# Graph attention on one core: gathering rows of x in place of a prepared node table, with the gates found per chunk

## The chip, the cores and the metric

The kernel runs on one core of one Trainium2 chip. The metric is the device time of one execution in microseconds (us). The engines are named as the profile names them: PE is TensorE, DVE is VectorE, ACT is ScalarE, POOL is GpSimd and SP is the engine that issues most plain transfers. Two runs of the kernel before took 2842.83 and 2848.6 us, median 2845.72 us.

## The reference, cut to what matters

There are 12,500 nodes with 128 features each and 212,500 edges, sorted by their target node. Each edge has a node whose features it carries (`col`, from dst) and a node into which it is pooled (`row`, from src).

```python
messages = x[col]                                   # 212500 x 128
gate = messages @ W_gate.T + b_gate                 # one number for an edge
h = messages @ W_lin.T + b_lin
g = gate[:, 0]
e = exp(g - segment_max(g, row)[row])
denom = segment_sum(e, row) + 1e-16
pooled = segment_sum((e / denom[row])[:, None] * h, row)
x = layernorm(x + pooled @ W_out.T + b_out)
```

The gate of an edge depends on its carried node alone: it is the same for all edges that carry that node. The kernel before uses this and finds 12,500 gates once. The changed kernel finds one for every gathered row.

## The kernel before, in words

**Keys and sort (about 0 to 480 us).** SP loads src and dst. DVE packs each edge into one 32-bit key, counts the edges of each block of 128 nodes by one-hot matmuls, adds pad keys so that each block is a whole number of tiles of 128 edges, and sorts 128 x 1792 keys by a bitonic network on DVE (lines 743 to 764 are its exchanges, two instructions each). Between phases the keys are transposed: PE transposes (L542), ACT copies the result back from PSUM (L441), and DVE goes on with the copy. ACT handles these copies in program order, behind whatever it was given earlier.

**The node table (beside the sort).** SP loads x into `nodes_sb` (L278). POOL multiplies ten nodes a partition at a time by the gate vector `wg` (L362, ten instructions), ACT sums each product row with an activation whose accumulator is read out (L430, 100 of them, a drain behind each), and adds the gate bias (L434). SP stores rows of 130 floats (128 features, a one, the gate; 520 bytes) to `node_table` in HBM (L282). In ACT's program all this stands ahead of the first copy L441. POOL then blanks the sums (L367).

**The chunk loop.** 1757 tiles of 128 edges are handled in 44 chunks of T = 40 tiles. For chunk i:
- DVE's `prepare(i + 1)` (L702 to L725) unpacks the next chunk's keys, PE transposes them (L552 to L557), and ACT's `copy_prep` (L444 to L450) puts the gather indices `gather_at` and the places into SBUF.
- POOL issues 40 indirect DMAs (L375), one per tile, each of which gathers 128 rows. It waits for `prep_copied` of that chunk and for `gather_buf_free`, since there are two buffers `gathered_rows`, used in turn.
- PE waits for the chunk's rows, then transposes the 40 columns of gates (L572). DVE runs a segmented max over them and forms the exponents (`softmax`, L890 to L912), with small transposes on PE in between, and ACT takes the exponential (`weigh`, L454).
- `add_tiles` (L941): for each tile DVE spreads the weights into a 128 x 128 matrix (L916), PE multiplies it with the gathered rows and their column of ones (L590), and DVE adds the 129 columns into the sums (L922). Four tiles make a batch, and the adds run two batches behind the spreads.

DVE's program is one row of work: `prepare(i + 1)`, `softmax(i)`, `add_tiles(i)`, `prepare(i + 2)`, and so on. The last chunk is handled in two parts of 16 and 24 tiles (`EARLY` = 16). The number of tiles is a bound: what is left over behind the real edges and their pads is filled with the key `LAST_KEY`, whose carried node is node 0.

**The end.** DVE forms the inverse denominators (L986 to L993). Then, in 14 groups of 7 blocks, POOL scales (L399), PE transposes and multiplies with the folded weights (L634), DVE adds x and takes mean and variance, and ACT normalises (L488). SP loads x and stores the result.

Of the kernel before, what the change touches and what calls it, by code (L numbers as in the profile page):

```python
# [78 lines left out]
def check_shapes():  # L79
    assert P * MAIN_COLS + REST_ROWS * REST_COLS == EDGES and NODE_ROWS * NODE_COLS == NODES  # L80
# [9 lines left out]
def graph_attention(nc, x, src, dst, w_lin, b_lin, w_gate, b_gate, w_out, b_out, out):  # L90
    check_shapes()
    with ExitStack() as ctx:
# [22 lines left out]
        gathered_rows = [arena[:, k * T * ROW:(k + 1) * T * ROW].rearrange("p (t f) -> p t f", f=ROW) for k in range(2)]  # L115
        gate_prod = sb("gate_prod", [P, GATE_COLS, FEAT])
        gate_junk = sb("gate_junk", [P, FEAT])
        gate_sum = sb("gate_sum", [P, NODE_COLS])
# [60 lines left out]
        free_at = 2 * T * ROW  # L179
# [17 lines left out]
        gate_rows = bank[4][0:T, 0:P]  # L197
# [73 lines left out]
        def _(sp):  # L271
# [12 lines left out]
            sp.dma_start(skeys[0:1].rearrange("(a n) -> a n", a=1), zero_key[:, :]).then_inc(keys_stored, 16)  # L284
            sp.dma_start(skeys[1 + KEYS:].rearrange("(p n) -> p n", n=P), iota_i[0:TAIL_ROWS, :]).then_inc(keys_stored, 16)
# [125 lines left out]
        def _(act):  # L411
# [643 lines left out]
```

## Time and profile before

| | us |
|---|---|
| median of the two runs | 2845.72 |
| span of the profiled execution | 2844.9 |
| POOL busy | 1748.5 (61%) |
| DVE busy | 1676.2 (59%) |
| PE busy | 1008.8 (35%) |
| ACT busy | 174.1 (6%) |
| gathers L375, 1757 of them, busy | 1675.1, mean 953 ns |
| spreads L916, 1760 of them, busy | 599.0 |
| adds L922, 1760 of them, busy | 605.6 |

The runs are given as whole times, and the profile gives the profiled execution's span, from its first to its last instruction: 2844.9 us, which is 0.8 us below the median of the runs. Busy shares are averages over three stages that have different limits, so they say little alone: DVE is close to full during the sort and at about half in the loop, where POOL is the engine that never rests for longer than 0.3 us. "Idle before" in a row is the time in which that engine did nothing ahead of the instruction, with what ended it behind the arrow. A name with q (DVEq, ACTq) is an engine's sequencer, here a drain that signals.

### The profile page before, as it was taken

Reading aid. Unit: us, or ns where it says so; the run is one execution under the profiler, and the core shown is the slowest. Engines: PE = TensorE matmul, PEld = TensorE weight load, DVE = VectorE, ACT = ScalarE, POOL = GpSimd, SP = SyncE. Lnnn points to the kernel's source line nnn. Section 1 sums busy time; section 2 is a strip of 40 time slices with the busy share of each in tenths; the row PEclk is TensorE's granted clock in tenths of the full one; section 3 lists DMA queues with packets and bytes.
Section 4 is the critical chain, followed back from the end, with each engine's and each line's share of the span. In section 5 each row is a group of like instructions: output and inputs, shape, how many; then the busy total and the mean of one; then the engine's idle time right before and its main releaser. Section 6 shows DMA issues by size and latency. Waiting matters only on the chain.

```text
span 2844.9 us, 25631 instructions
## 1 busy us (share of the span) xinstructions
PE 1008.8 (35%) x5080; PEld 835.6 (29%) x5080; DVE 1676.2 (59%) x5604; ACT 174.1 (6%) x664; POOL 1748.5 (61%) x1792
## 2 busy tenths in 40 slices
PE   3012112225233342433334243342433424333377
PEld 3011111224232232422323233232333323233255
DVE  9969998346455464645546455464655646455454
ACT  0421110000000000000000000000000000000025
POOL 0411002777777777777777777777777777777621
PEclk9999996565566665566656556565655656566566
DMA  3020001222222222222222222222222222223924
GB/s 115 3 92 0 0 0 29 54 54 54 55 53 55 53 55 54 54 55 53 55 53 54 54 54 54 54 53 55 53 55 54 55 53 54 54 54 67 41 50 122
DMA packets 91745, 148.65 MB, mean 52 GB/s; under 512 B 30393, under 2 KB 61970, under 8 KB 91588
## 3 DMA queue, kind: packets, MB, share of 16 engines
q0 software_dynamic: 56224, 117.06, 20.8%
q1 hardware_dynamic: 34767, 31.04, 3.5%
q10 hardware_dynamic: 722, 0.20, 0.0%
q8 instruction: 12, 0.20, 0.0%
q14 instruction: 20, 0.16, 0.0%
HBM read 134.35 MB, written 13.83 MB: 52 GB/s over the span
## 4 chain that ended last, share of the span: by engine, by line
POOL 43%; issue 23%; DVE 17%; PE 7%; DVEq 2%; another core or an unknown queue 2%; ACT 2%; DMA 2%; ACTq 1%; POOLq 0%
POOL arena L375 42%; DVE spread L916 3%; DVE nodes_sb L922 2%; PE bank L590 2%; PE bank L634 2%; DMA arena<-node_table,gather_at 1%; DVE rows_b L751 1%; DVE rows_a L750 1%; DVE rows_a L751 1%; POOL gate_prod L362 1%; DVE rows_b L750 1%; ACT gate_junk L430 1%; DVEq L952 1%; DVE turn_b L751 1%
## 5 line engine op out<-in xcount | busy, mean ns | idle before, releaser
L375 POOL DMA_INDIRECT arena<-node_table,gather_at x1757 | 1675.1, 953 | 790.6 <-issue 530.3
L590 PE MATMUL bank<-arena,spread 128*128 128x129 f32 x3520 | 736.9, 379 | 334.5 <-DVE nodes_sb L922 220.6
L590 PEld LDWEIGHTS bank<-arena,spread 128*128 128x128 f32 x3520 | 642.8, 276 | 424.5 <-DVE nodes_sb L922 291.4
L916 DVE TENSOR_SCALAR spread<-iota_row,place_t,weights 128x128 f32<-128x128 f32 x1760 | 599.0, 357 | 184.7 <-PE bank L590 83.0
L922 DVE SCALAR_TENSOR_TENSOR nodes_sb<-nodes_sb,weights,bank 128x129 f32 x1760 | 605.6, 344 | 55.2 <-PE bank L590 10.5
L894 DVE TENSOR_TENSOR_SCAN run_max<-pen,bank 40x128 f32<-40x128 f32 (+1 forms) x45 | 18.5, 411 | 756.8 <-PE bank L572 756.8
L572 PE MATMUL bank<-ident,arena 128*40 128x128 f32 (+1 forms) x45 | 17.3, 384 | 703.0 <-DMA arena<-node_table,gather_at 703.0
L572 PEld LDWEIGHTS bank<-ident,arena 128*40 128x40 f32 (+1 forms) x45 | 5.4, 119 | 711.0 <-issue 711.0
L552 PE MATMUL bank<-ident,dst_f 40*128 40x40 f32 x44 | 13.1, 297 | 235.7 <-DVEq L725 234.2
L542 PE MATMUL bank<-ident,rows_a 128*128 128x128 f32 x112 | 28.1, 429 | 180.0 <-DVE rows_a L776 144.7
L446 ACT ACTIVATE gather_at<-bank 128x40 int32<-128x40 f32 x44 | 8.9, 203 | 1258.6 <-PE bank L557 1229.2
L399 POOL TENSOR_TENSOR turn_a<-nodes_sb,arena 128x896 f32 (+1 forms) x14 | 23.7, 1697 | 97.2 <-PE bank L626 51.0
L552 PEld LDWEIGHTS bank<-ident,dst_f 40*128 40x128 f32 x44 | 7.9, 179 | 245.1 <-issue 245.1
L542 PEld LDWEIGHTS bank<-ident,rows_a 128*128 128x128 f32 x112 | 21.7, 223 | 186.3 <-DVE rows_a L776 149.4
L751 DVE TENSOR_TENSOR rows_a<-rows_b 128x384 f32<-128x384 f32 (+1 forms) x108 | 71.8, 665 | 0.0
L750 DVE TENSOR_TENSOR rows_b<-rows_a 128x384 f32<-128x384 f32 (+1 forms) x108 | 67.1, 621 | 5.9 <-ACT rows_a L441 4.6
L750 DVE TENSOR_TENSOR rows_a<-rows_b 128x384 f32<-128x384 f32 (+1 forms) x108 | 69.6, 644 | 1.7
L751 DVE TENSOR_TENSOR rows_b<-rows_a 128x384 f32<-128x384 f32 (+1 forms) x108 | 69.4, 642 | 0.0
L454 ACT ACTIVATE weights<-bank 128x80 f32<-128x80 f32 (+2 forms) x45 | 10.6, 236 | 935.2 <-PE bank L582 935.2
L362 POOL TENSOR_TENSOR gate_prod<-nodes_sb,wg 125x1280 f32<-125x1280 f32 x10 | 37.2, 3721 | 43.5 <-ACTq L433 43.5
L634 PE MATMUL bank<-wc_t,arena 128*128 128x128 f32 x196 | 60.1, 398 | 4.6 <-ACTq L477 4.6
L542 PE MATMUL bank<-ident,turn_b 128*128 128x128 f32 x98 | 24.3, 428 | 97.7 <-DVE turn_b L751 97.7
(161 smaller groups left out, 1066.0 us busy)
## 6 DMA issues: line engine op xcount, KB each, us to landing
arena<-node_table,gather_at POOLq DMA_INDIRECT x1757, 20.6
node_table<-nodes_sb SPq DMA_DIRECT2D x1, 6347.7 KB
nodes_sb<-in_x SPq DMA_DIRECT2D x1, 6250.0 KB
rows_a<-in_x SPq DMA_DIRECT2D x13, 448.0 KB, 4.1
out<-rows_b SPq DMA_DIRECT2D x13, 448.0 KB, 3.3
k<-sorted_keys SPq DMA_DIRECT2D x132, 20.0 KB
turn_a<-in_src SPq DMA_DIRECT2D x1, 828.0 KB
turn_b<-in_dst SPq DMA_DIRECT2D x1, 828.0 KB
```

Of the source, the lines that this page charges most:

```text
L362: pool.tensor_tensor(gate_prod[0:NODE_ROWS], node_rows[:, c * GATE_COLS:(c + 1) * GATE_COLS, 0:FEAT], wg[0:NODE_ROWS].unsqueeze(1).to_broa ...
L375: pool.indirect_dma_start(out=gathered_rows[par][:, t, :], out_offset=None, in_=table[:, :], in_offset=bass.IndirectOffsetOnAxis(ap=gather ...
L399: pool.tensor_tensor(pooled[par][:, :, :], here[:, :, 0:FEAT], inv_den[:, bass.ds(g * GB, GB)].unsqueeze(2).to_broadcast([P, GB, FEAT]), A ...
L430: last = act.activation(gate_junk[0:NODE_ROWS], gate_prod[0:NODE_ROWS, n, :], ACT.Copy, accum_out=gate_sum[0:NODE_ROWS, at:at + 1])
L542: last = pe.transpose(ps[:, q:q + P], from_[:, at + q:at + q + P], ident[:, :])
L590: last = pe.matmul(tile_ps(slot), lhsT=spread[:, slot, :], rhs=gathered_rows[par][:, b * BATCH + u, 0:WIDTH], start=True, stop=True)
L634: pe.matmul(to, lhsT=pooled_t[par][:, c, :], rhs=wc_t[:, :], start=True, stop=False)
L750: dve.tensor_tensor(vb[:, :, 0, :], va[:, :, 0, :], va[:, :, 1, :], ALU.min)
L751: step_ends(g, dve.tensor_tensor(vb[:, :, 1, :], va[:, :, 0, :], va[:, :, 1, :], ALU.max))
L916: return dve.tensor_scalar(spread[:, slot, :], iota_row[:, :], place_t[par][:, t:t + 1], weights[par][:, 0, t:t + 1], ALU.is_equal, ALU.mult)
L922: dve.scalar_tensor_tensor(here, here, weights[par][:, 1, t:t + 1], tile_ps(slot), ALU.mult, ALU.add).then_inc(sums_added, 1)
L952: got = nc.values_load_multi_w_load_instructions(offs[par][0:1, b * BATCH:b * BATCH + n], engines=[mybir.EngineType.DVE], min_val=0, max_v ...
```

## The change

The node table is gone: its load, products, sums, bias, store and the waits on them. The gathers read rows of x itself, 512 bytes each. Since these rows have no gate and no one in them, the buffers' column of ones is written once (L349 of the changed kernel), and the gates of a chunk are found when its rows have landed. DVE multiplies all 40 x 128 elements a partition by the gate vector, which it has copied to PSUM, in one instruction (`find_gates`). ACT sums each tile's 129 elements (the 129th is the gate bias, written once) by an activation with an accumulator, with a drain behind each, 40 a chunk (`sum_gates`). PE then transposes the sums where it transposed the gathered column before. The wait for the rows moves from PE to DVE.

```diff
-        table = nc.dram_tensor("node_table", (NODES, ROW), F32).ap()
...
+        gate_terms = arena[:, 14000:14000 + T * WIDTH].rearrange("p (t f) -> p t f", f=WIDTH)
+        gates = sb("gates", [P, T])
...
-            sp.dma_start(node_rows[:, :, 0:FEAT], x.rearrange("(p n) f -> p n f", n=NODE_COLS)).then_inc(x_loaded, 16)
-
-            sp.wait_ge(gates_ready, 1)
-            sp.wait_ge(ones_ready, 1)
-            sp.dma_start(table.rearrange("(p n) f -> p n f", n=NODE_COLS), node_rows).then_inc(table_stored, 16)
...
-            for c in range(NODE_COLS // GATE_COLS):
-                if c > 0:
-                    pool.wait_ge(prod_used, c)
-                pool.tensor_tensor(gate_prod[0:NODE_ROWS], node_rows[:, c * GATE_COLS:(c + 1) * GATE_COLS, 0:FEAT],
-                                   wg[0:NODE_ROWS].unsqueeze(1).to_broadcast([NODE_ROWS, GATE_COLS, FEAT]),
-                                   ALU.mult).then_inc(prod_ready, 1)
-
-            pool.wait_ge(table_stored, 16)
             pool.memset(sums, 0.0).then_inc(sums_blank, 1)
 
             pool.wait_ge(hist_ready, 1)
+            for par in range(2):
+                pool.memset(gathered_rows[par][:, :, FEAT:WIDTH], 1.0)
+            pool.drain().then_inc(ones_ready, 1)
...
-                    pool.indirect_dma_start(out=gathered_rows[par][:, t, :], out_offset=None, in_=table[:, :],
+                    pool.indirect_dma_start(out=gathered_rows[par][:, t, 0:FEAT], out_offset=None, in_=x[:, :],
...
-            for c in range(NODE_COLS // GATE_COLS):
-                act.wait_ge(prod_ready, c + 1)
-                for n in range(GATE_COLS):
-                    at = c * GATE_COLS + n
-                    last = act.activation(gate_junk[0:NODE_ROWS], gate_prod[0:NODE_ROWS, n, :], ACT.Copy,
-                                          accum_out=gate_sum[0:NODE_ROWS, at:at + 1])
-                    act.drain()
-                act.drain().then_inc(prod_used, 1)
-            act.activation(node_rows[:, :, FEAT + 1], gate_sum[0:NODE_ROWS, :], ACT.Identity,
-                           bias=bg[0:NODE_ROWS, 0:1]).then_inc(gates_ready, 1)
+            act.wait_ge(hist_ready, 1)
+            act.activation(gate_terms[:, :, FEAT], bg[:, 0:1].to_broadcast([P, T]), ACT.Copy).then_inc(bias_placed, 1)
...
+            def sum_gates(i, at, n):
+                act.wait_ge(terms_ready, i + 1)
+                for t in range(at, at + n):
+                    act.activation(gate_junk[:, :], gate_terms[:, t, :], ACT.Copy, accum_out=gates[:, t:t + 1])
+                    act.drain()
+                act.drain().then_inc(gates_found, 1)
...
                     copy_prep(2 * j + (par + 1), 1 - par)
+                    sum_gates(2 * j + par, 0, T)
                     weigh(2 * j + par, par)
...
+                pe.wait_ge(gates_found, i + 1)
                 pe.nop(nofuse=True)
-                pe.transpose(gate_rows[0:n], gathered_rows[par][:, 0:n, FEAT + 1], ident[:, :]).then_inc(gates_turned, 1)
+                pe.transpose(gate_rows[0:n], gates[:, 0:n], ident[:, :]).then_inc(gates_turned, 1)
...
-                    pe.wait_ge(rows_gathered[par], 16 * T * j + 16 * T)
...
+            dve.tensor_copy(wg_ps, wg[:, :])
...
+            def find_gates(par, at, n):
+                dve.tensor_tensor(gate_terms[:, at:at + n, 0:FEAT], gathered_rows[par][:, at:at + n, 0:FEAT],
+                                  wg_ps.unsqueeze(1).to_broadcast([P, n, FEAT]), ALU.mult)
+                dve.drain().then_inc(terms_ready, 1)
...
                     prepare(i + 1, j + par, 1 - par)
+                    dve.wait_ge(rows_gathered[par], 16 * T * j + 16 * T)
+                    find_gates(par, 0, T)
                     softmax(i, par)
                     add_tiles(i, i + 1, par, range(NB))
```

Two places show how the engines' instructions stand. The first is DVE at the seam between `prepare(i + 1)` and `softmax(i)` in the loop, before:

```order
L723 TENSOR_SCALAR pen<-differs 40x256
L724 TENSOR_SCALAR goes_on<-pen_tile 40x1
L894 SCALAR_TENSOR_TENSOR run_max<-pen,bank 40x128
L897 SCALAR_TENSOR_TENSOR carry<-tile_pen,carry,bank 1x40
L900 COPY carry_col<-bank 40x1
```

and the same place now:

```order
L706 TENSOR_SCALAR pen<-differs 40x256
L707 TENSOR_SCALAR goes_on<-pen_tile 40x1
L963 ISA
L877 TENSOR_TENSOR arena<-arena,bank 128x40x128
L885 SCALAR_TENSOR_TENSOR run_max<-pen,bank 40x128
L888 SCALAR_TENSOR_TENSOR carry<-tile_pen,carry,bank 1x40
L891 COPY carry_col<-bank 40x1
```

The product over a whole chunk stands between the two, ahead of the scan, and behind it the scan waits for ACT and PE. The second place is ACT in the loop, half an iteration, before:

```order
L446 ACTIVATE gather_at<-bank 128x40
L447 ACTIVATE place_t<-bank 128x40
L448 ACTIVATE offs<-bank 1x40
L449 ACTIVATE tile_pen<-bank 1x40
L453 REGISTER_ALU
L454 ACTIVATE weights<-bank 128x80
```

and now:

```order
L419 ACTIVATE gather_at<-bank 128x40
L420 ACTIVATE place_t<-bank 128x40
L421 ACTIVATE offs<-bank 1x40
L422 ACTIVATE tile_pen<-bank 1x40
L426 REGISTER_ALU
L428 ACTIVATE gate_junk,gates<-arena 128x129 x40
L434 ACTIVATE weights<-bank 128x80
```

Forty summing activations stand between the copies of the next chunk's indices, which they do not delay, and the exponential of this chunk.

## Rows read from the trace of the kernel before

**Rows 1.** The page, part 4: the chain that ended last, by engine
```profile
POOL 43%; issue 23%; DVE 17%; PE 7%; DVEq 2%; another core or an unknown queue 2%; ACT 2%; DMA 2%; ACTq 1%; POOLq 0%
```
**Rows 2.** Timeline of a chunk (start, length, engine, line, idle before and its releaser)
```profile
1234.58 0.39 PE L572 MATMUL bank<-ident,arena 128*40 128x128 f32 x1 [15.50 <-DMA arena<-node_table,gather_at]
1235.00 0.41 DVE L894 TENSOR_TENSOR_SCAN run_max<-pen,bank 40x128 f32<-40x128 f32 x1 [16.73 <-PE bank L572]
...
1265.59 0.35 DVE L706 TENSOR_SCALAR node_i<-k 40x384 int32<-40x384 int32 x1
...
1268.31 0.14 DVE L724 TENSOR_SCALAR goes_on<-pen_tile 40x1 f32<-40x1 f32 x1
...
1269.46 0.18 ACT L449 ACTIVATE tile_pen<-bank 1x40 f32<-1x40 f32 x1
...
1282.06 0.94 POOL L375 DMA_INDIRECT arena<-node_table,gather_at  x1 [0.30 <-issue]
1283.31 0.94 POOL L375 DMA_INDIRECT arena<-node_table,gather_at  x1 [0.30 <-issue]
...
1284.71 0.38 PE L572 MATMUL bank<-ident,arena 128*40 128x128 f32 x1 [15.55 <-DMA arena<-node_table,gather_at]
1285.13 0.41 DVE L894 TENSOR_TENSOR_SCAN run_max<-pen,bank 40x128 f32<-40x128 f32 x1 [16.69 <-PE bank L572]
```
**Rows 3.** Timeline of the table's first products: ACT's sums, and POOL behind ten of them
```profile
77.90 0.31 ACT L430 ACTIVATE gate_junk<-gate_prod 125x128 f32<-125x128 f32 x1 [61.48 <-POOL gate_prod L362]
78.12 0.19 ACT L430 ACTIVATION_READ_ACCUMULATOR gate_junk<-gate_prod 125x1 f32 x1
78.38 0.31 ACT L430 ACTIVATE gate_junk<-gate_prod 125x128 f32<-125x128 f32 x1
...
82.67 2.91 POOL L362 TENSOR_TENSOR gate_prod<-nodes_sb,wg 125x1280 f32<-125x1280 f32 x1 [4.87 <-ACTq L433]
```
**Rows 4.** Timeline of DVE in the sort: first, second and last stretched instruction, and a wait
```profile
74.72 0.56 DVE L750 TENSOR_TENSOR rows_a<-rows_b 128x384 f32<-128x384 f32 x1
75.19 3.03 DVE L751 TENSOR_TENSOR rows_a<-rows_b 128x384 f32<-128x384 f32 x1
...
82.98 3.02 DVE L744 TENSOR_TENSOR rows_b<-rows_a 128x384 f32<-128x384 f32 x1
...
130.46 3.16 DVE L776 TENSOR_SCALAR rows_a<-rows_a,flips 128x1024 f32<-128x1024 f32 x1
...
161.98 0.69 DVE L750 TENSOR_TENSOR turn_b<-turn_a 128x512 f32<-128x512 f32 x1 [25.71 <-ACT turn_a L441]
```
**Rows 5.** Waits of DVE between 200 and 480 us (total, times, longest)
```profile
DVE turn_b L750 <- ACT turn_a L441: 1.3, 3, 0.8
```
**Rows 6.** Timeline of DVE late in the sort: a product-like instruction on 512 elements
```profile
456.91 0.69 DVE L750 TENSOR_TENSOR rows_a<-rows_b 128x512 f32<-128x512 f32 x1
```
**Rows 7.** The page, part 5: instructions with an operand in PSUM (busy, mean ns)
```profile
L922 DVE SCALAR_TENSOR_TENSOR nodes_sb<-nodes_sb,weights,bank 128x129 f32 x1760 | 605.6, 344 | 55.2 <-PE bank L590 10.5
```
**Rows 8.** Timeline: the gates' transpose of chunks 0, 41 and 42
```profile
530.69 0.38 PE L572 MATMUL bank<-ident,arena 128*40 128x128 f32 x1 [32.48 <-DMA arena<-node_table,gather_at]
...
2593.63 0.38 PE L572 MATMUL bank<-ident,arena 128*40 128x128 f32 x1 [16.43 <-DMA arena<-node_table,gather_at]
...
2650.14 0.38 PE L572 MATMUL bank<-ident,arena 128*40 128x128 f32 x1 [22.16 <-DMA arena<-node_table,gather_at]
```
**Rows 9.** Windows near the end (busy of each engine, clock, DMA share, GB/s)
```profile
2600.00:2620.00 20.00, 13.89 (x71) 12.38 (x72) 17.70 (x69) 0.00 (x0) 15.12 (x17) 0.76 0.24 53
...
2640.00:2650.00 10.00, 0.00 (x0) 0.00 (x0) 0.00 (x0) 0.00 (x0) 7.56 (x9) 0.50 0.97 40
```
**Rows 10.** Timeline from chunk 42 to the denominators
```profile
2670.45 2.74 PE L590 MATMUL bank<-arena,spread 128*128 128x129 f32 x12 [10.62 <-issue]
...
2711.76 0.41 DVE L894 TENSOR_TENSOR_SCAN run_max<-pen,bank 40x128 f32<-40x128 f32 x1 [3.88 <-PE bank L572]
...
2733.45 0.25 DVE L986 TENSOR_SCALAR arena<-nodes_sb 128x98 f32<-128x98 f32 x1
```

More of the change, by code:

```diff
@@ L68 @@
 WIDTH = FEAT + 1
-ROW = FEAT + 2
-NODE_ROWS, NODE_COLS = 125, 100
-GATE_COLS = 10
 NEG = -1.0e30
@@ L79, in check_shapes @@
 def check_shapes():
-    assert P * MAIN_COLS + REST_ROWS * REST_COLS == EDGES and NODE_ROWS * NODE_COLS == NODES
+    assert P * MAIN_COLS + REST_ROWS * REST_COLS == EDGES
     assert EARLY % BATCH == 0 and CHUNKS % 4 == 0 and (CHUNKS - 1) * T + EARLY < TILES <= CHUNKS * T and (CHUNKS + 1) * T * P < KEYS + TAIL_ROWS * P
@@ L108, in graph_attention @@
         lohi_b = turn_b.ap().bitcast(BF16)
-        nodes_sb = sb("nodes_sb", [P, 13000])
-        node_rows = nodes_sb[0:NODE_ROWS, 0:NODE_COLS * ROW].rearrange("p (n f) -> p n f", f=ROW)
-        sums = nodes_sb[:, 0:BLOCKS * WIDTH]
+        sums = sb("sums", [P, BLOCKS * WIDTH]).ap()
         arena = sb("arena", [P, 23 * EDGE_COLS // 2 + EDGE_COLS])
@@ L114, in graph_attention @@
         part2_i = arena[:, 23 * EDGE_COLS // 2:23 * EDGE_COLS // 2 + EDGE_COLS].bitcast(I32)
[L115 to L118, printed above, removed]
+        gathered_rows = [arena[:, k * T * WIDTH:(k + 1) * T * WIDTH].rearrange("p (t f) -> p t f", f=WIDTH) for k in range(2)]
+        gate_terms = arena[:, 14000:14000 + T * WIDTH].rearrange("p (t f) -> p t f", f=WIDTH)
+        gates = sb("gates", [P, T])
+        gate_junk = sb("gate_junk", [P, WIDTH])
         wg = sb("wg", [P, FEAT])
@@ L177, in graph_attention @@
         pooled_t = [arena[:, k * HALF:k * HALF + GB * P].rearrange("p (c f) -> p c f", f=P) for k in range(2)]
-        free_at = 2 * T * ROW
+        free_at = 2 * T * WIDTH
         inv_den = arena[:, free_at:free_at + BLOCKS]
@@ L196, in graph_attention @@
         count_ps = bank[6][:, 0:HI * LO]
-        gate_rows = bank[4][0:T, 0:P]
+        gate_rows, wg_ps = bank[4][0:T, 0:P], bank[4][:, 256:256 + FEAT]
         tile_block_ps, tile_pen_ps, tile_max_ps = bank[6][0:1, 256:256 + T], bank[6][0:1, 384:384 + T], bank[5][0:1, 128:128 + T]
@@ L204, in tile_ps @@
             return bank[slot // 2][:, (slot % 2) * 256:(slot % 2) * 256 + WIDTH]
-        src_loaded, dst_loaded, x_loaded, weights_loaded = sem("src_loaded"), sem("dst_loaded"), sem("x_loaded"), sem("weights_loaded")
+        src_loaded, dst_loaded, weights_loaded = sem("src_loaded"), sem("dst_loaded"), sem("weights_loaded")
         iotas_ready, consts_ready = sem("iotas_ready"), sem("consts_ready")
-        prod_ready, prod_used, gates_ready, ones_ready = sem("prod_ready"), sem("prod_used"), sem("gates_ready"), sem("ones_ready")
-        table_stored, keys_stored, zero_ready = sem("table_stored"), sem("keys_stored"), sem("zero_ready")
+        terms_ready, gates_found, ones_ready, bias_placed = sem("terms_ready"), sem("gates_found"), sem("ones_ready"), sem("bias_placed")
+        keys_stored, zero_ready = sem("keys_stored"), sem("zero_ready")
         onehots_ready, hist_ready, spread_ready, counts_ready = sem("onehots_ready"), sem("hist_ready"), sem("spread_ready"), sem("counts_ready")
@@ L344, in _ @@
             sp.wait_ge(stored[1], 16 * (GROUPS // 2 + 1))
-            sp.wait_ge(table_stored, 16)
         @block.gpsimd
@@ L464, in _ @@
                     copy_prep(2 * j + (par + 1), 1 - par)
+                    sum_gates(2 * j + par, 0, T)
                     weigh(2 * j + par, par)
             copy_prep(CHUNKS - 1, 1)
+            sum_gates(CHUNKS - 2, 0, T)
             weigh(CHUNKS - 2, 0)
+            sum_gates(CHUNKS - 1, 0, EARLY)
             weigh(CHUNKS - 1, 1, slice(0, EARLY))
+            sum_gates(CHUNKS, EARLY, T - EARLY)
             weigh(CHUNKS, 1, slice(EARLY, T))
@@ L886, in _ @@
             dve.wait_ge(sums_blank, 1)
+            dve.wait_ge(bias_placed, 1)
+            dve.wait_ge(weights_loaded, 16 * 6)
+            dve.tensor_copy(wg_ps, wg[:, :])
             dve.drain().then_inc(sums_added, 2 * BATCH)
+            def find_gates(par, at, n):
+                dve.tensor_tensor(gate_terms[:, at:at + n, 0:FEAT], gathered_rows[par][:, at:at + n, 0:FEAT],
+                                  wg_ps.unsqueeze(1).to_broadcast([P, n, FEAT]), ALU.mult)
+                dve.drain().then_inc(terms_ready, 1)
             def softmax(i, par, n=T):
@@ L974, in _ @@
             prepare(CHUNKS - 1, CHUNKS // 2 - 1, 1)
+            dve.wait_ge(rows_gathered[0], 16 * T * (CHUNKS // 2))
+            find_gates(0, 0, T)
             softmax(CHUNKS - 2, 0)
             add_tiles(CHUNKS - 2, CHUNKS - 1, 0, range(NB))
+            dve.wait_ge(rows_gathered[1], 16 * T * (CHUNKS // 2 - 1) + 16 * EARLY)
+            find_gates(1, 0, EARLY)
             softmax(CHUNKS - 1, 1, EARLY)
             add_tiles(CHUNKS - 1, CHUNKS, 1, range(EARLY // BATCH))
+            dve.wait_ge(late_gathered, 16 * (TILES - (CHUNKS - 1) * T - EARLY))
+            find_gates(1, EARLY, T - EARLY)
             softmax(CHUNKS, 1)
```

8 lines of the change are left out of this document (2 added, 6 removed).

## The prediction

> **What bounds the kernel now.** I read the chain of waits first. It lies on POOL for 43% and on "issue" for 23% [rows 1]; issue is mostly POOL's 0.30 us between two gathers. So in the loop the pace is POOL's: one gather every 1.25 us, 40 in a chunk, and the reader is to see in [rows 2] that nothing holds it up at a chunk's boundary. Chunk 0's gates are transposed at 530.69 and chunk 41's at 2593.63 [rows 8], which is 50.32 us a chunk.
>
> Then the timeline of one chunk, for what the other engines have to spare. From L894 at 1235.00 to L894 at 1285.13 DVE takes 50.13 us, of which it waits 16.69 for rows; the other 33.44 are its own path (softmax, spreads and adds with their short waits, then `prepare`). More telling is what POOL needs from that path: the indices of chunk i+2 are copied at 1269.46 + 0.18 = 1269.64, and the next chunk's first gather is at 1283.31. The loop has a slack of 13.7 us a chunk. Anything added between landing and `add_tiles` is free up to there, and not beyond.
>
> Third, the sort, where DVE is the pace: it waits 25.71 us once for ACT's first copy, since ACT is busy with the table's sums until then, and some instructions take 3.03 in place of 0.56 us [rows 4].
>
> **What the change removes.** The wait of 25.71 goes, since ACT has only one small instruction ahead of its first copy. Late in the sort such waits are 1.3 us in three [rows 5], so 0.4 stays: 25.3 gained. The stretched instructions number seven, 75.19 the first and 130.46 the last; each begins within half a microsecond of one of POOL's products or runs up to its end, as the one at 82.98 beside the product at 82.67 [rows 3, 4]. Five of 384 elements lose 3.03 - 0.56 = 2.47 us, and I take this for all seven: 17.3 gained. POOL's other work moves early and blocks nobody that waits: the sums are not needed before the loop. Together the loop starts 42.6 us earlier, less about 0.2 for copying the gate vector to PSUM: **42.4**. The bound below is 25 (if the stretching had another cause), above 45. The load of x and the store of the table are hidden by the sort, and cost nothing either way. So chunk 0's rows are there at 530.69 - 42.4 = 488.3.
>
> **What it adds in each chunk**, all in a row between landing and the gates' transpose:
> - The product: 512 elements take 0.69 [rows 6], 384 take 0.56 [rows 4], so 1.02 ns an element and 0.17 fixed; 5120 elements take **5.4**. One operand lies in PSUM. The nearest rows with one are the adds, 344 ns for 129 elements [rows 7], which fit 0.17 + 0.13 plus 0.04; nothing there is slower by the element, but they are too short to exclude it. Bounds 5.3 and, at half the pace, 10.7.
> - The sums: ACT starts one at 77.90 and the next at 78.38; ten with their handover back to POOL take 82.67 - 77.90 = 4.77 [rows 3]. These are the same instruction, accumulator read and drain, on 128 elements instead of 129. Forty take **18.9**. Bounds: if read and drain went on beside the next activation, 0.22 each (78.12 - 77.90), 8.8; if each met a hiccup of 0.1, 23.
> - Handovers DVE to ACT and ACT to PE: about **0.3** over the DMA to PE of before; the transpose's 0.42 (1234.58 to 1235.00) stood inside DVE's wait, and now counts.
>
> DVE's path becomes 33.44 + 0.42 + 5.4 + 18.9 + 0.3 = **58.5 us** a chunk. All but 13.7 of the added 24.6 would be past the slack; but once DVE is late the loop has another law. Gathers of chunk i+2 start when its indices are copied, 1.2 us behind the path's end, and 40 gathers later, 39 x 1.25 + (1284.71 - 1282.06) = 51.4, the rows are there. That ring spans two chunks, so it allows (58.5 + 1.2 + 51.4) / 2 = 55.6 us a chunk. DVE's own path, 58.5, is longer, so it decides: the rows of the next chunk lie there when DVE comes, POOL waits some 8 us a chunk, and the kernel changes from bound by POOL to bound by the chain DVE, ACT, PE, DVE. That gathers might get cheaper with 512 bytes instead of 520 is then worth nothing, and that they might be slowed by up to 5 us a chunk by the product costs nothing.
>
> The Trainium skill, page "ScalarE: Activation LUTs", section "What ACT_TABLE_LOAD costs", puts an activation with immediate scale and bias at 186 ns + 0.833 ns an element, with 93 ns of overlap back to back. By that, 129 elements are an estimated 200 ns and forty 8.0 us, the path would be 47.6, and the loop would keep POOL's pace. The rows above have 0.48 us from start to start, because the accumulator's read and the drain stand between; the page prices neither.
>
> **The loop.** Chunk 42's product starts at 488.3 + 42 x 58.5 = 2945.3.
>
> **The end of the loop.** Before, from chunk 42's transpose to L986 it took 2733.45 - 2650.14 = 83.3 [rows 8, 10]. In it were 3.9 of waiting for the last rows, which go, and 10.6 in which PE stood at "issue" in the middle of chunk 42 [rows 10]. Both go with DMA queues that are full from about 2630: share 0.97 at only 40 GB/s where it was 0.24 at 53 [rows 9]. These are the filler tiles, where all 128 rows of a gather are node 0. Their gathers still come, 37 of them in chunk 43, when DVE begins chunk 42, so I let the 10.6 stand. 128 x 520 bytes at 40 GB/s are 1.7 us a gather, 63 us for them: landed at 2945.3 + 1.2 + 66 = 3013, ahead of their use near 3037. The gates add 24.6 for chunk 42; for 16 tiles 2.3 + 7.6 + 0.3 = 10.2; for 24 tiles 3.3 + 11.4 + 0.3 = 15.0. So 83.3 - 3.9 + 49.8 = 129.2, and L986 is at 3074.5. Behind it nothing changes: 2844.9 - 2733.45 = 111.4.
>
> **Sum:** 3074.5 + 111.4 = 3185.9, against 2844.9 of the same execution: +341. The median of the runs is 0.8 above that span, so 3187 us, 12% slower.
>
> **Rivals.**
> *The sums overlap, and POOL stays the pace* (the other side). If read and drain were hidden, forty sums would be 8.8 and DVE's path 48.4; the ring gives (48.4 + 52.6) / 2 = 50.5 a chunk, 0.2 over today's. It decides at a path of 48.0, which is an added 14. The 42.4 of the sort are gained, 42 x 0.2 = 8 lost, and the end of the loop, where rows of node 0 gate the last part, loses some 29 (the added parts of 24.6, 10.2 and 15.0, less 10.1, 4.0 and 6.1 of hidden reads). About 2841 us, no change. For it: the rule above. Against: the ten sums in 4.77 us, the same instructions. 5%; another 2% that the gain shows, and it is over 2% faster.
> *The product is slow in PSUM, or ACT's sums are slower in the loop than in the prologue.* At half pace the product adds 5.3 a chunk, and hiccups of 0.1 add 4: 44 x 5 = 220, about 3400 us. For it: the price with a long PSUM operand is not in the trace. Against: the adds, and that ACT's sums ran beside DVE and POOL in the table too. 9%.
> *The gathers from x don't bring the rows at the pace of the table's,* so that the ring decides at 58.5 or more: they would have to take 5.8 us a chunk longer. Nothing speaks for it; rows of 512 bytes are less data. 2%.
> *The forecast,* 82%: its own terms give 3155 (no stall of PE, 0.5 us a chunk less) to 3260 (the gain of the sort only 25, 1.3 us a chunk more in handovers and small waits).
>
> The range 3150 to 3265 leaves out 2 in 10. A difference of 2% is 57 us and about what counts as a change here. Slower: 82 + 9 + 2 = 93%; within 2%: 5%; faster: 2%.
>
> **What would show it.** In the profile after: L877 about 5.4 us; L428 at 0.47 us a tile and 18.9 a chunk, ACT busy near 1000 us; DVE waiting for the scan some 20 us a chunk, now for ACT's sums and not for rows; POOL idle about 8 us a chunk behind the index copy; the first gather near 436 in place of 478; no stretched DVE instructions before 135. A chunk pace of 50.5 would make the first rival right, and one of 62 or more the second. What would make me wrong is above all a term of the 58.5, since each tenth of a microsecond in it is worth 4.

## The result

| | kernel before | changed kernel |
|---|---|---|
| median of the runs, us | 2845.72 (2 runs) | 3204.02 (2 runs) |
| ratio, with its 95% interval | 1 | 1.1257 (1.1233 to 1.1281) |
| span of the profiled execution, us | 2844.9 | 3203.2 |
| first gather, us from the start | 478 | 442.2 |
| pace of the loop, us a chunk | 50.32 | 58.60 |
| POOL busy | 61% | 53% |
| ACT busy | 6% | 26% |

The changed kernel is 12.6% slower. The forecast was 3187 us with a range of 3150 to 3265, so it was 17 us too low.

### The profile page after: what moved, and what is told of

Read it like the earlier page. It is cut to its first block, busy times and chain, and to the rows that moved or that the text cites. A ratio compares the mean times of both kernels' runs of the same rounds, so it can differ in the third digit from the quotient of the medians.

```text
span 3203.2 us, 30726 instructions
## 1 busy us (share of the span) xinstructions
PE 997.6 (31%) x5080; PEld 827.3 (26%) x5080; DVE 1908.9 (60%) x5650; ACT 843.4 (26%) x3984; POOL 1707.3 (53%) x1783
## 4 chain that ended last, share of the span: by engine, by line
DVE 37%; issue 23%; ACT 17%; PE 9%; DVEq 6%; ACTq 5%; POOL 2%; DMA 0%; POOLq 0%
ACT gate_junk L428 16%; DVE spread L907 7%; DVE arena L877 7%; DVE sums L913 5%; PE bank L577 5%; ACTq L429 5%; DVEq L943 3%; POOL arena L356 2%; DVE rows_a L733 2%; DVE rows_b L734 2%; DVE rows_a L734 2%; DVE rows_b L733 2%; PE bank L617 1%; DVE turn_b L734 1%; DVE turn_b L733 1%
## 5 line engine op out<-in xcount | busy, mean ns | idle before, releaser
L356 POOL DMA_INDIRECT arena<-in_x,gather_at x1757 | 1670.9, 951 | 1275.1 <-ACTq L423 751.4
L428 ACT ACTIVATE gate_junk<-arena 128x129 f32<-128x129 f32 x1760 | 549.4, 312 | 407.9 <-DVEq L879 278.2
L913 DVE SCALAR_TENSOR_TENSOR sums<-sums,weights,bank 128x129 f32 x1760 | 605.6, 344 | 54.4 <-PE bank L577 10.3
L885 DVE TENSOR_TENSOR_SCAN run_max<-pen,bank 40x128 f32<-40x128 f32 (+1 forms) x45 | 18.5, 412 | 869.6 <-PE bank L559 869.6
L559 PE MATMUL bank<-ident,gates 128*40 128x128 f32 (+1 forms) x45 | 16.9, 375 | 1102.9 <-ACTq L430 1102.9
L428 ACT ACTIVATION_READ_ACCUMULATOR gate_junk<-arena 128x1 f32 x1760 | 327.8, 186 | 0.0
L877 DVE TENSOR_TENSOR arena<-arena,bank 128x5120 f32<-128x5120 f32 (+2 forms) x45 | 241.6, 5370 | 43.8 <-DMA arena<-in_x,gather_at 37.2
L380 POOL TENSOR_TENSOR turn_a<-sums,arena 128x896 f32 (+1 forms) x14 | 23.7, 1699 | 142.1 <-DVEq L988 90.8
L536 PE MATMUL bank<-ident,dst_f 40*128 40x40 f32 x44 | 13.1, 297 | 233.0 <-DVEq L708 231.4
L414 ACT ACTIVATE turn_a<-bank 128x512 f32<-128x512 f32 (+1 forms) x40 | 20.7, 543 | 232.8 <-PE bank L526 232.8
L733 DVE TENSOR_TENSOR rows_a<-rows_b 128x384 f32<-128x384 f32 (+1 forms) x108 | 67.1, 621 | 1.7
L434 ACT ACTIVATE weights<-bank 128x80 f32<-128x80 f32 (+2 forms) x45 | 10.6, 236 | 216.1 <-PE bank L569 216.1
L734 DVE TENSOR_TENSOR rows_a<-rows_b 128x384 f32<-128x384 f32 (+1 forms) x108 | 66.6, 617 | 0.0
```

The costliest lines, as they stand in the source:

```text
L356: pool.indirect_dma_start(out=gathered_rows[par][:, t, 0:FEAT], out_offset=None, in_=x[:, :], in_offset=bass.IndirectOffsetOnAxis(ap=gathe ...
L428: act.activation(gate_junk[:, :], gate_terms[:, t, :], ACT.Copy, accum_out=gates[:, t:t + 1])
L733: dve.tensor_tensor(vb[:, :, 0, :], va[:, :, 0, :], va[:, :, 1, :], ALU.min)
L734: step_ends(g, dve.tensor_tensor(vb[:, :, 1, :], va[:, :, 0, :], va[:, :, 1, :], ALU.max))
L877: dve.tensor_tensor(gate_terms[:, at:at + n, 0:FEAT], gathered_rows[par][:, at:at + n, 0:FEAT], wg_ps.unsqueeze(1).to_broadcast([P, n, FEA ...
L913: dve.scalar_tensor_tensor(here, here, weights[par][:, 1, t:t + 1], tile_ps(slot), ALU.mult, ALU.add).then_inc(sums_added, 1)
```

## The profile after

The page's line of busy times, its chain of waits (part 4) and five of its groups (part 5: busy, mean ns of one, idle before and its releaser):

```profile
PE 997.6 (31%) x5080; PEld 827.3 (26%) x5080; DVE 1908.9 (60%) x5650; ACT 843.4 (26%) x3984; POOL 1707.3 (53%) x1783
...
DVE 37%; issue 23%; ACT 17%; PE 9%; DVEq 6%; ACTq 5%; POOL 2%; DMA 0%; POOLq 0%
...
L356 POOL DMA_INDIRECT arena<-in_x,gather_at x1757 | 1670.9, 951 | 1275.1 <-ACTq L423 751.4
...
L428 ACT ACTIVATE gate_junk<-arena 128x129 f32<-128x129 f32 x1760 | 549.4, 312 | 407.9 <-DVEq L879 278.2
...
L913 DVE SCALAR_TENSOR_TENSOR sums<-sums,weights,bank 128x129 f32 x1760 | 605.6, 344 | 54.4 <-PE bank L577 10.3
L885 DVE TENSOR_TENSOR_SCAN run_max<-pen,bank 40x128 f32<-40x128 f32 (+1 forms) x45 | 18.5, 412 | 869.6 <-PE bank L559 869.6
...
L877 DVE TENSOR_TENSOR arena<-arena,bank 128x5120 f32<-128x5120 f32 (+2 forms) x45 | 241.6, 5370 | 43.8 <-DMA arena<-in_x,gather_at 37.2
```

Read the chain first, against [rows 1]: POOL held 43% of it and now holds 2%. DVE has 37% and ACT, which took no part in the loop's pace, 17%. POOL's gathers cost what they did (951 ns, 953 before). What is new is the idle time ahead of them, 751.4 us released by ACT's index copy. DVE no longer waits for rows: of the 43.8 us ahead of the product, 37.2 are chunk 0's. It waits 869.6 us at the scan L885 instead, and the releaser PE leads on to ACT. The adds L913 have their old 344 ns: DVE's other work did not get slower.

The waits from 700 to 2900 us (in total, times, longest) show the same by the chunk:

```profile
DVE run_max L885 <- PE bank L559: 723.2, 37, 19.5
POOL arena L356 <- ACTq L423: 327.9, 38, 9.2
```

That is 19.5 us of DVE a chunk, and 8.6 us of POOL. The timeline of one chunk, to be laid beside [rows 2]:

```profile
1490.81 5.49 DVE L877 TENSOR_TENSOR arena<-arena,bank 128x5120 f32<-128x5120 f32 x1
1491.44 0.20 ACT L419 ACTIVATE gather_at<-bank 128x40 int32<-128x40 f32 x1 [29.39 <-PE bank L541]
1492.70 0.95 POOL L356 DMA_INDIRECT arena<-in_x,gather_at  x1 [8.01 <-ACTq L423]
...
1500.13 0.31 ACT L428 ACTIVATE gate_junk<-arena 128x129 f32<-128x129 f32 x1
1500.35 0.19 ACT L428 ACTIVATION_READ_ACCUMULATOR gate_junk<-arena 128x1 f32 x1
1500.61 0.31 ACT L428 ACTIVATE gate_junk<-arena 128x129 f32<-128x129 f32 x1
...
1515.43 0.37 PE L559 MATMUL bank<-ident,gates 128*40 128x128 f32 x1 [24.02 <-ACTq L430]
1515.84 0.41 DVE L885 TENSOR_TENSOR_SCAN run_max<-pen,bank 40x128 f32<-40x128 f32 x1 [19.54 <-PE bank L559]
...
1549.53 5.49 DVE L877 TENSOR_TENSOR arena<-arena,bank 128x5120 f32<-128x5120 f32 x1 [0.20 <-issue]
```

The product starts as soon as `prepare` is done: its rows lie there. Then all 40 sums run, 0.47 us each, while DVE and PE stand still, and 24.6 us after the product's start (1490.81 to 1515.43) the gates are transposed. The next product starts after 58.72 us. POOL gets its indices 0.6 us into the product and waits 8.01 for them.

## The experiments

Ratios are against the kernel before, run again beside each group of experiments on the same chip. Its medians there were 2841.07 (the first four experiments), 2842.34 (the next four) and 2844.33 us (the last two); whole times of different groups are compared only roughly. Two theories were to be told apart first: mine, that the path DVE, ACT, PE, DVE sets 58.5 us a chunk and each part of the gates' 24.6 us counts, against a rival in which gathers from x, not the gates, had made the loop slow.

**e1, no gates.** Product, sums and the wait for them are left out. The gates stay zero, so the weights of a target's edges are all equal.

```diff
-                    sum_gates(2 * j + par, 0, T)
...
-                pe.wait_ge(gates_found, i + 1)
...
+                    pe.wait_ge(rows_gathered[par], 16 * T * j + 16 * T)
...
-                    dve.wait_ge(rows_gathered[par], 16 * T * j + 16 * T)
-                    find_gates(par, 0, T)
```

> The changed kernel without its product and its sums: the gates stay zero, so the attention weights are all equal; the table is gone and 512-byte rows of x are gathered as in the change. Theory (the loss is the serial work between landing and the gates' transpose, and nothing else in the change costs): the loop is POOL's again at 50.3 us a chunk, the first gather stays at 442, which is 36 us ahead of the kernel before, and the end of the loop is as before: 2846 - 36 = 2810 us. Rival (gathers from x are slower than from the table, or the moved waits cost): a pace above 50.6 us a chunk and over 2825 us.

Measured: 2805.17 us (2 runs), ratio 0.9871 (0.9852 to 0.9891), 50.36 us a chunk. The page, part 5:

```profile
L356 POOL DMA_INDIRECT arena<-in_x,gather_at x1757 | 1677.0, 954 | 916.9 <-issue 527.2
```

From its first gather on POOL is back to waiting for nothing but its own issue. The gathers from x keep the table's pace, and that rival falls. The run also prices the two halves of the change. Up to the denominators (2733.45 us before, 2699.07 here, 3096.06 in the changed kernel) leaving out the table gains 34.4 us, and the gates lose 397.0. The whole spans differ by 42.5 and 400.8, but 8.1 of the 42.5 lie behind the denominators, where the code is the same (see "Behind it nothing changes" in the account of the prediction). The medians of the runs side by side give 35.9.

**e2, every second sum.** ACT sums 20 of the 40 tiles, which leaves half the gates at zero (the code blanks them once).

```diff
-                for t in range(at, at + n):
+                for t in range(at, at + n, 2):
```

> ACT sums every second tile only; the other gates stay zero. Theory (two limits: DVE's serial path, and a ring over two chunks of path + 52.6): the path falls from 58.7 to 58.7 - 20 x 0.47 = 49.3, and the ring gives (49.3 + 52.6) / 2 = 51.0 us a chunk; in the end of the loop 19 us less than in the changed kernel, some 7 more for landing behind slow filler gathers: about 2866 us. Rival (only the larger of DVE's path and POOL's own 50.3 counts, no ring): a pace of 50.3, and 2838 us. Rival (the sums are not what the loop waits for): 3204 us stays.

Measured: 2885.77 us (2 runs), ratio 1.0155 (1.0135 to 1.0175), 51.49 us a chunk. The timeline, three transposes in a row, and between them two products with the first and the fortieth gather of a chunk:

```profile
1535.85 0.38 PE L559 MATMUL bank<-ident,gates 128*40 128x128 f32 x1 [15.45 <-ACTq L430]
...
1588.32 0.37 PE L559 MATMUL bank<-ident,gates 128*40 128x128 f32 x1 [17.73 <-ACTq L430]
...
1623.55 5.49 DVE L878 TENSOR_TENSOR arena<-arena,bank 128x5120 f32<-128x5120 f32 x1 [1.37 <-DMA arena<-in_x,gather_at]
1624.28 0.94 POOL L356 DMA_INDIRECT arena<-in_x,gather_at  x1 [2.27 <-ACTq L423]
...
1638.66 0.37 PE L559 MATMUL bank<-ident,gates 128*40 128x128 f32 x1 [15.68 <-ACTq L430]
...
1673.26 0.94 POOL L356 DMA_INDIRECT arena<-in_x,gather_at  x1 [0.30 <-issue]
1675.75 5.49 DVE L878 TENSOR_TENSOR arena<-arena,bank 128x5120 f32<-128x5120 f32 x1 [3.35 <-DMA arena<-in_x,gather_at]
```

The path is 58.6 - 20 x 0.47 = 49.2 here, shorter than POOL's 50.3, and still the loop takes 51.5. That is the ring over two chunks: it alternates between 52.5 and 50.3 us, and POOL waits 2.27 once in two chunks. The law is right and its constant was too small. 2 x 51.49 - 49.2 = 53.8, where I had 1.2 + 51.4 = 52.6. These rows show most of the missing 1.2. DVE's path ended at 1623.55 - 1.37 = 1622.18, and the first gather starts 2.10 later, where I had 1.2. The fortieth gather starts 48.98 behind it, where I had 48.75, and the next product 2.49 behind that, where I had 2.65. Together that is 53.6. The run took 20 us more than expected, which is about the 0.49 a chunk over 42 chunks.

**e3, no drain between the sums.** The activation writes its output over its own input instead of `gate_junk`, so nothing has to be waited for between two of them.

```diff
-                    act.activation(gate_junk[:, :], gate_terms[:, t, :], ACT.Copy, accum_out=gates[:, t:t + 1])
-                    act.drain()
+                    act.activation(gate_terms[:, t, :], gate_terms[:, t, :], ACT.Copy, accum_out=gates[:, t:t + 1])
```

> All 40 sums, but without the drain behind each; each activation writes back over its own input in place of a shared scratch row. Theory (the drain and the accumulator's read stand between two activations, 0.47 us from start to start): without the drain 0.40 at best if the read still stands between (0.31 + 0.19 less overlap), a path of 55.9 and 3080 us; if the drain alone held it up, 0.22 each, a path of 48.7, a pace of 50.6 and about 2850 us. Rival (it is the read, not the drain): 0.47 stays and so does 3204 us.

Measured: 2932.26 us (2 runs), ratio 1.0319 (1.0298 to 1.0339), 52.73 us a chunk. The timeline of ACT:

```profile
1500.50 0.29 ACT L428 ACTIVATE arena<-arena 128x129 f32<-128x129 f32 x1
1500.70 0.19 ACT L428 ACTIVATION_READ_ACCUMULATOR arena<-arena 128x1 f32 x1
1500.79 0.29 ACT L428 ACTIVATE arena<-arena 128x129 f32<-128x129 f32 x1
```

From start to start it is 0.29 us, against 0.47 above, which is between the two values that I expected (0.40 and 0.22). So the drain was 0.18 of each sum. The read starts 0.20 behind its activation and takes 0.19, and the next activation starts 0.10 before the read's end. Forty sums are 7.1 shorter, and the ring with the constant measured in e2 gives ((58.6 - 7.1) + 53.8) / 2 = 52.7, as measured. The first rival of the prediction needed 0.22 a sum, and even without drains it is not reached.

**e4, POOL's blanking late.** The prediction let POOL's moved work block nobody. The trace after shows POOL and DVE in the first microseconds otherwise:

```profile
1.65 10.63 POOL L345 MEMSET sums<- 128x12642 f32 x1 [0.16 <-issue]
...
3.20 9.17 DVE L641 CAST iota_row<-iota_i 128x128 f32<-128x128 int32 x1
3.29 9.07 DVE L642 CAST part_idx<-part_idx_i 128x1 f32<-128x1 int32 x1
3.36 9.04 DVE L643 TENSOR_SCALAR diag_eq<-diag_i 64x64 f32<-64x64 int32 x1
...
14.05 1.03 DVE L662 TENSOR_SCALAR rows_b<-turn_a 128x1696 int32<-128x1696 int32 x1
```

Two conversions and a comparison take 9 us, and all end with POOL's memset, at 12.3. They stand one behind the other on DVE, so the rows show that the first was held; the other two may only have stood behind it. In the kernel before the memset stood behind the table, at 211 us. The experiment moves it behind POOL's wait for the histogram:

```diff
-            pool.memset(sums, 0.0).then_inc(sums_blank, 1)
             pool.wait_ge(hist_ready, 1)
+            pool.memset(sums, 0.0).then_inc(sums_blank, 1)
```

> The changed kernel, but POOL blanks the sums behind its wait for the histogram, during the sort's exchanges with two inputs. Theory (the 10.6 us blanking at 1.65 blocked three small DVE instructions until 12.3, and the key packing began at 14.05 instead of 7.16; the same blanking did not stretch the exchanges at 211 us in the kernel before): the first gather at 435.3 instead of 442.2, 6.9 us less, 3197 us. Rival (blanking blocks DVE wherever it stands): no gain, or up to 10 us more.

Measured: first gather at 435.4 instead of 442.2. The median is 3198.75 us (4 runs), ratio 1.1259 (1.124 to 1.1278), which does not tell it from the changed kernel's 1.1257. The gain is shown by the trace alone: chunk 0's product starts at 487.34 instead of 494.27. At the denominators 4.7 us of it are left, since PE's stall in chunk 42 is 13.1 here and 9.85 there. The timeline:

```profile
3.20 0.18 DVE L640 CAST iota_row<-iota_i 128x128 f32<-128x128 int32 x1
...
7.11 1.04 DVE L661 TENSOR_SCALAR rows_b<-turn_a 128x1696 int32<-128x1696 int32 x1 [1.83 <-DMA turn_a<-in_src]
...
52.15 10.63 POOL L346 MEMSET sums<- 128x12642 f32 x1 [50.66 <-PE bank L509]
53.25 0.69 DVE L732 TENSOR_TENSOR rows_b<-rows_a 128x512 f32<-128x512 f32 x1
```

DVE's key packing starts 6.9 us earlier. The same memset beside two-input exchanges of the sort stretches none of them: 0.69 us, as in [rows 6]. The rival, that blanking blocks DVE wherever it stands, falls. The Trainium skill, page "SBUF — State Buffer", section "Who interferes with whom", says that a DVE instruction with two SBUF inputs contends with a GpSimd instruction that reads SBUF, and not with one that only writes it, and that casts and tensor-scalar operations can enter modes that contend. These rows agree with both: the table's products, which read, stretched exchanges to 3.03 us [rows 4], and the memset, which only writes, stretches none.

**e5, the sums on DVE.** One reduction over 40 x 129 elements behind the product, nothing on ACT.

```diff
-                    sum_gates(2 * j + par, 0, T)
...
-                dve.drain().then_inc(terms_ready, 1)
+                dve.drain()
+                dve.tensor_reduce(gates[:, at:at + n], gate_terms[:, at:at + n, :], AX.X, ALU.add)
+                dve.drain().then_inc(gates_found, 1)
```

> The changed kernel, but DVE sums the products itself, with one reduction over the 40 x 129 elements behind the product, and ACT sums nothing. Theory (two limits; the ring's constant is 53.8 by the two runs with fewer or quicker sums): the reduction takes 5.5 like the product, the path is 58.6 - 24.6 + 11.2 = 45.2, the ring allows (45.2 + 53.8) / 2 = 49.5, so POOL's 50.4 a chunk decides. Against the kernel without any gates (2805 us) only the end of the loop grows, by 11.2 + 4.7 + 6.9 = 23 us: 2828 us, just under the kernel before. Rival (a reduction of 5160 elements with an SBUF input keeps GpSimd from writing descriptors): gathers longer than 0.97 us on the mean and a pace above 51, 2870 us or more.

Measured: 2820.12 us (5 runs), ratio 0.992 (0.9906 to 0.9933), 50.30 us a chunk. The page, part 5:

```profile
L356 POOL DMA_INDIRECT arena<-in_x,gather_at x1757 | 1674.0, 953 | 920.1 <-issue 533.0
...
L876 DVE TENSOR_REDUCE gates<-arena 128x40 f32<-128x5160 f32 (+2 forms) x45 | 243.4, 5408 | 3.3
```

A full chunk's reduction takes 5.5 us on DVE (the mean, 5.41, has the last chunk's two shorter ones in it) and does what took 18.9 on ACT. The path is some 45 us, inside POOL's 50.3, and the sort's gain shows. No gather is lengthened (953 ns), so the rival falls. So the changed kernel's loss is the form of the sums, not the per-row gates as such.

**e6, the gate vector read from SBUF.** What is the copy in PSUM good for?

```diff
-                                  wg_ps.unsqueeze(1).to_broadcast([P, n, FEAT]), ALU.mult)
+                                  wg[:, :].unsqueeze(1).to_broadcast([P, n, FEAT]), ALU.mult)
```

> The changed kernel, but the product reads the gate vector from SBUF, not from its copy in PSUM, so that it has two inputs in SBUF. Theory (the loop is bound by DVE's path; POOL has some 8 us a chunk to spare): the product still takes 5.49, or 5.4 without PSUM's latency; POOL may be held up to 5.5 us a chunk beside it, which is hidden; 3204 us within 5. Rival (POOL's gathers block the product as its products blocked the exchanges): the product takes up to 0.9 us longer for each gather beside it, a path of 60 to 62, 3260 to 3350 us.

Measured: 3203.55 us (4 runs), ratio 1.1274 (1.1257 to 1.1291), 58.62 us a chunk. The timeline of one chunk:

```profile
1491.10 5.49 DVE L877 TENSOR_TENSOR arena<-arena,wg 128x5120 f32<-128x5120 f32 x1
1492.99 4.42 POOL L356 DMA_INDIRECT arena<-in_x,gather_at  x1 [4.78 <-ACTq L423]
1497.71 0.94 POOL L356 DMA_INDIRECT arena<-in_x,gather_at  x1 [0.30 <-issue]
```

The product itself costs the same, 5.49, so the rival, a product stretched by gathers, falls. The first gather of a chunk that runs into it takes 4.42 us instead of 0.95 and ends 0.8 behind it; POOL's wait shrinks from 8.0 to 4.8 in return. Nothing is lost while POOL has slack. The Trainium skill, page "SBUF — State Buffer", section "Who interferes with whom", also infers that such a two-input product leaves descriptor writing alone; here it holds a gather's issue, and the measurement decides. A gather also reads its indices from SBUF, which would put it under that section's rule on instructions that read; no run separates the reading from the writing.

**e7, the kernel before with other filler nodes.** This is for the stall that I let stand, 10.62 of PE at "issue" [rows 10]. Filler and pad keys carry nodes spread over 0 to 12416 instead of node 0; beside the few instructions that write them nothing changes.

```diff
+            pool.iota(pad_node[:, :], [[1, BLOCKS]], base=0, channel_multiplier=BLOCKS - 1)
...
+            dve.tensor_tensor(keys_here, keys_here, pad_node[:, 0:PAD_AT - MAIN_COLS], ALU.bitwise_or)
...
+            dve.tensor_tensor(pads_here, pads_here, pad_node[:, :], ALU.bitwise_or)
```

> The kernel before; pad and filler keys carry the nodes 0 to 12416 in place of node 0 alone, so that the last 48 gathers read 128 different rows each. Theory (128 reads of one row make a gather take 1.7 us, which delays landing by 6, the last part by 4, and PE's next instructions by 10): DMA share near 0.25 instead of 0.97 from 2630 on, no stall of PE at 2660, and 20 us less: 2822 us. Rival (the queues are full at the end for another reason): share 0.9 stays and so does the time.

Measured: 2820.27 us (5 runs), ratio 0.9923 (0.991 to 0.9937). A window near the end, and the instruction that had stalled:

```profile
2650.00:2670.00 20.00, 15.19 (x72) 13.60 (x72) 17.79 (x69) 0.00 (x0) 15.13 (x17) 0.67 0.21 54
...
2653.50 3.07 PE L592 MATMUL bank<-arena,spread 128*128 128x129 f32 x12 [0.47 <-issue]
```

The same window in the kernel before:

```profile
2650.00:2670.00 20.00, 4.12 (x17) 3.45 (x18) 6.70 (x25) 0.24 (x1) 15.12 (x17) 0.50 0.94 41
```

DMA share 0.21 instead of 0.94 at more bytes a second (54 and 41 GB/s), DVE busy 17.79 of 20 us instead of 6.70, and the stall is 0.47. So both came from the 128 reads of one row. A stall of DVE of 2.3 us stays, at 2628.7.

**e8, the changed kernel with the same filler nodes.** The edit is that of e7.

> The changed kernel with the same edit of pad and filler keys. Theory (in the changed kernel the rows are there in time, and the full queues cost only through stalls at issue: 8.7 on ACT, 9.9 on PE, 2.9 on DVE): these three go, 21 us less, 3180 us. Rival (the stalls are those of code run for the first time behind the loop, whatever the queues do): the stalls stay and the time too.

Measured: 3188.51 us (5 runs), ratio 1.1225 (1.1209 to 1.124), which is 8.5 us above the expectation. The stall that had hit ACT, in the changed kernel and here:

```profile
2985.39 0.31 ACT L428 ACTIVATE gate_junk<-arena 128x129 f32<-128x129 f32 x1 [8.66 <-issue]
```
```profile
2976.85 0.31 ACT L430 ACTIVATE gate_junk<-arena 128x129 f32<-128x129 f32 x1 [2.37 <-issue]
```

It shrinks from 8.66 to 2.37, PE's later stall is gone, and a small one of DVE stays (2.20; 2.85 in the changed kernel). What feeds these small ones is open: for them the rival, code that runs for the first time, is not excluded. From chunk 42's product to the denominators it takes 121.45 us instead of 137.53, so 16.1 of the expected 21 us show there.

**e9, the parts that help together:** the edits of e5, e4's late blanking and e8's filler nodes in one kernel.

> Three edits of the changed kernel together: DVE sums the products, POOL blanks the sums behind the histogram, pad and filler keys carry different nodes. Theory (they add up: 2820 for DVE's sums, 7 less for the blanking, and 22 less for the keys as in the kernel before): first gather at 435.3, a pace of 50.3, 2791 us, which beats both kernels and the kernel before with its keys spread (2820). Rival (the start and the end are hidden by each other's waits): 2800 or more.

Measured: 2802.10 us (4 runs), ratio 0.9852 (0.9836 to 0.9869), first gather at 435.6, 50.30 us a chunk. The timeline of DVE:

```profile
1493.61 5.49 DVE L880 TENSOR_TENSOR arena<-arena,bank 128x5120 f32<-128x5120 f32 x1 [4.71 <-DMA arena<-in_x,gather_at]
1499.17 5.53 DVE L883 TENSOR_REDUCE gates<-arena 128x40 f32<-128x5160 f32 x1
```

This beats both kernels (the kernel before by 1.5%), though the expectation was 11 us better. It had added up gains measured one by one. e5 gives 22.2 by its median and e7 22.1, which with the blanking's 6.9 is 51.2, and e9 gives 42.2. The traces of e5 and e9 show where the rest is missing. Chunk 0's product starts 6.3 us earlier (493.99 and 487.67), so the blanking's gain is there. But from that product to the denominators e9 saves only 7.4 us (2212.8 and 2205.5), where the same keys saved 21.4 in the kernel before (2733.45 and 2712.09). e5 had less to lose there: its stalls at "issue" are 5.12 of DVE and 2.94 of PE, where PE's in the kernel before is 10.62. DVE waits 4.7 us a chunk for rows, so the loop leaves nothing more to gain on DVE.

**e10, e9 with the gate vector in SBUF.** The edit of e6 again, on a kernel in which POOL is the pace.

```diff
-                                  wg_ps.unsqueeze(1).to_broadcast([P, n, FEAT]), ALU.mult)
+                                  wg[:, :].unsqueeze(1).to_broadcast([P, n, FEAT]), ALU.mult)
```

> The same, but the product reads the gate vector from SBUF. With the changed kernel this held one gather a chunk for 4.4 us and cost nothing. Theory (here POOL sets the pace, so what it is held up counts in full): 3.5 to 5.2 us more a chunk, a pace of 54 to 55.5, 2790 + 43 x 4.3 = 2975 us, 2940 to 3020. Rival (POOL catches up between chunks or isn't held, since it is in the middle of a row of gathers): within 20 us of the other.

Measured: 2976.44 us (4 runs), ratio 1.0471 (1.0453 to 1.0488), 54.46 us a chunk. The timeline:

```profile
1522.32 5.49 DVE L880 TENSOR_TENSOR arena<-arena,wg 128x5120 f32<-128x5120 f32 x1 [8.97 <-DMA arena<-in_x,gather_at]
1523.48 5.15 POOL L357 DMA_INDIRECT arena<-in_x,gather_at  x1 [0.30 <-issue]
1527.88 5.53 DVE L883 TENSOR_REDUCE gates<-arena 128x40 f32<-128x5160 f32 x1
1528.93 0.94 POOL L357 DMA_INDIRECT arena<-in_x,gather_at  x1 [0.30 <-issue]
```

One gather a chunk takes 5.15 instead of 0.94, and the pace rises by 54.46 - 50.30 = 4.16 us: the hold-up counts in full. The reduction has one SBUF input and holds nothing. The same edit cost nothing in e6 and 174 us here.

## Why the prediction was right, and where it missed

The mechanism of the loop held: POOL's pace gives way to the path DVE, ACT, PE, DVE, the ring is shorter than the path, and the loop loses 8.3 us a chunk. Of the 17.3 us between the predicted span, 3185.9, and the measured 3203.2, each has its place:

| step of the prediction | predicted | measured | adds to the span |
|---|---|---|---|
| chunk 0's product starts | 488.3 | 494.27 | +6.0 |
| from there to chunk 42's product | 2457.0 | 2464.26 | +7.3 |
| from there to the denominators | 129.2 | 137.53 | +8.3 |
| from there to the end | 111.4 | 107.1 | -4.3 |

- **The sort: mis-sized, by one step.** The wait of 25.71 and the stretched exchanges went as predicted. But "POOL's other work moves early and blocks nobody that waits" was wrong. I asked who waits for the memset's result and not who runs beside it, and 6.9 of the 42.4 were lost (e4). With the blanking late the product starts at 487.34, where the prediction had 488.3.
- **The product** takes 5.49, predicted 5.4, at full pace from PSUM. e6 and e10 show what that operand saves.
- **The sums:** 0.47 a tile, predicted 0.47. From product to transpose it is 24.6, predicted 24.6. Summing like instructions of the table's code gave the figure; e3 gives its parts.
- **The path:** 58.60, predicted 58.5, which is 4.2 over 42 chunks; another 2.85 is DVE's stall at 2957.36. The ring would have been 56.2 with its measured constant, still shorter. With a path below 53.8 it would have decided, and my constant would then have made the pace 0.6 a chunk too low.
- **The end of the loop: mis-sized.** I let PE's stall of 10.6 stand, and it came (9.85). I did not ask which other engine might stall in the new place: ACT lost 8.66 in the middle of chunk 42's sums. In the changed kernel, a window there and PE's own stall:

```profile
2970.00:2990.00 20.00, 0.00 (x0) 0.00 (x0) 0.00 (x0) 9.78 (x50) 15.12 (x17) 0.50 0.96 39
...
3011.20 2.74 PE L577 MATMUL bank<-arena,spread 128*128 128x129 f32 x12 [9.85 <-issue]
```

- **"Behind it nothing changes"** held within 4.3 us, and the direction is luck. The windows from the denominators to the end, before and after (busy of each engine, granted clock, DMA share, GB/s):

```profile
2733.45:2844.93 111.48, 91.41 (x406) 64.83 (x406) 55.56 (x256) 57.82 (x154) 23.72 (x14) 0.69 0.39 107
```
```profile
3096.06:3203.20 107.14, 87.15 (x406) 61.93 (x406) 55.62 (x256) 57.86 (x154) 23.74 (x14) 0.72 0.40 112
```

The same 406 instructions of PE take 4.3 us less, and the granted TensorE clock, a mix of its two levels (1.2 and 2.4 GHz), is 0.72 of full speed on the mean instead of 0.69. In the profile of e1 this stretch takes 103.3 us at 0.78, in that of e5 112.2 at 0.70. So up to 9 us between two spans can come from a stretch in which the edit changed nothing. What sets the mix was not tested.
- **Signs that I named:** POOL's wait near 8 (8.6), DVE's near 20 (19.5), no exchange stretched, all seen. ACT "busy near 1000" was wrong, 843.4: the read overlaps its activation by 0.09 us and the drain is not counted as busy, so of each 0.47 only 0.40 show.
- **The rivals.** Overlapping sums are excluded by the rows and by e3. A product slow in PSUM is excluded at 5.49. Slow gathers from x are excluded by e1.

## What to carry to other kernels

Before work is moved off a table and into a loop, find the slack between the path of each engine and the pace, here 13.7 us a chunk. 11 us of added work (e5) were free and 24.6 cost 8.3 a chunk, because 40 small accumulating activations took 18.9 where one reduction took 5.5. When an instruction moves, ask who runs beside it in its new place as well as who waits for it. A hold-up of an engine with slack costs nothing until another edit takes the slack away: the same operand choice was worth 0 and 174 us.

## What was not expected of the hardware

- A memset on POOL that only writes held a small one-input conversion on DVE, and the two instructions behind it, for 9 us, to the memset's end. It held no two-input exchange (e4).
- A DVE product with both inputs in SBUF held one indirect gather's issue to 4.4 or 5.2 us; with one operand in PSUM, and by a reduction, none was held (e6, e10).
- Gathers whose 128 rows are one and the same row keep the DMA engines at a share of 0.96 for 39 GB/s, and while they do, PE, ACT or DVE stands at "issue" for up to 16 us at a place that no semaphore explains (8.66 of ACT and 9.85 of PE in the changed kernel, 10.62 of PE in the kernel before, 6.65 of DVE and 16.19 of ACT in e2). With different rows the share is 0.21 at 54 GB/s, and no stall in these stretches is longer than 2.4 us (e7, e8).
- In each of the changed kernel's two long stalls one transfer runs that the profile calls "instruction" (queue, packets, MB, share, from the windows 2976.5 to 2985.4 and 3001 to 3011.2):

```profile
q14 instruction: 1, 0.01, 0.2%
```
```profile
q8 instruction: 1, 0.02, 0.6%
```

They start at 2983.74 and 3008.94, and the engines go on 1.7 and 2.3 us later. In e7 such a transfer starts at 2651.12, 2.4 us before PE goes on at 2653.50, and PE has stood still for 0.47 only. That the transfers queued behind the gathers fits this and is not shown: the trace has no time at which they were asked for.
